# Mamba layer of a four-layer tower: two of sixteen state weightings moved to GpSimd, with their sums taken two places later

## The reference

```python
dbl = u @ xproj_w.T
delta = jax.nn.softplus(dbl[..., :DT_RANK] @ dt_w.T + dt_b)
A = -jnp.exp(A_log)
def step(hst, ins):                      # along the sequence
    d_t, B_t, C_t, u_t = ins
    dA = jnp.exp(d_t[..., None] * A)
    hst = dA * hst + (d_t * u_t)[..., None] * B_t[:, None, :]
    y = jnp.einsum('bds,bs->bd', hst, C_t)
    return (hst, y)
y = y + u * Dp
return (y * jax.nn.silu(z)) @ out_w.T
```

## Time and profile before

| | us |
|---|---|
| median of three runs | 3469.69 |
| lowest and highest run | 3464.54, 3469.84 |
| the profiled execution's own time | 3465.39 |
| its span | 3463.6 |
| the scan loop of the stage (first scan to last weighting) | 654.65 to 1364.65 |
| VectorE busy in the whole span | 2402.1 (69%) |
| TensorE busy in the whole span | 2484.2 (72%) |
| ScalarE, GpSimd busy in the whole span | 1594.3, 830.5 |
| mean granted TensorE clock | 0.826 of full speed |

### The profile page before, as it was taken

The page is one execution under the profiler, slowest core; times in us unless marked ns, Lnnn a source line. Parts: engine busy times, 40 slices in busy tenths (PEclk is TensorE's granted clock), DMA queues, the critical chain, the costliest instruction groups (busy, mean ns, idle before and its releaser), DMA issues. The chain is left out here.

```text
span 3463.6 us, 38446 instructions
## 1 busy us (share of the span) xinstructions
PE 2484.2 (72%) x12628; PEld 1541.3 (44%) x12668; DVE 2402.1 (69%) x5684; ACT 1594.3 (46%) x2912; POOL 830.5 (24%) x414
## 2 busy tenths in 40 slices
PE   4967995788888887589951112588889778885457
PEld 4964663333434333379840111322222456674335
DVE  5464336399999998411268998688888699999531
ACT  3111112566666662211215774577878455554211
POOL 2000000477777774167500000000000011111022
PEclk9868997799999998699965555799999887787578
DMA  1121001101011110411100000144435400000221
GB/s 53 19 83 46 1 1 32 78 21 66 33 49 49 49 49 0 148 49 40 64 12 0 1 0 2 62 146 152 146 118 187 126 1 1 1 1 1 86 112 54
DMA packets 81794, 185.36 MB, mean 54 GB/s; under 512 B 35197, under 2 KB 52827, under 8 KB 76251
## 3 DMA queue, kind: packets, MB, share of 16 engines
q1 hardware_dynamic: 75452, 170.66, 14.8%
q0 software_dynamic: 6144, 12.25, 1.1%
HBM read 166.00 MB, written 24.77 MB: 55 GB/s over the span
## 5 line engine op out<-in xcount | busy, mean ns | idle before, releaser
L2072 POOL TENSOR_TENSOR mam_st<-mam_du,mam_b_rows 128x1536 f32<-128x1536 f32 x128 | 439.5, 3441 | 172.9 <-PE mam_ysum L2141 172.3
L2302 DVE TENSOR_TENSOR_SCAN mam_st<-mam_da,mam_st 128x512 f32<-128x512 f32 x384 | 441.1, 1204 | 35.9 <-ACT mam_da L2242 18.2
L2141 PE MATMUL mam_ysum<-mam_st,held_ident 128*128 128x512 f32 x768 | 390.0, 648 | 2.2 <-DVE mam_st L2308 2.2
L1708 ACT ACTIVATE cod_hp<-cod_up,cod_b 128x512 f32<-128x512 f32 x512 | 316.7, 703 | 83.6 <-PE cod_up L1569 83.5
L2242 ACT ACTIVATE mam_da<-mam_delta,mamw_decay 128x508 f32<-128x508 f32 x384 | 254.2, 683 | 184.2 <-DVE mam_st L2302 149.6
L2423 POOL TENSOR_TENSOR att_probs<-att_se,att_neg 128x1536 f32<-128x1536 f32 x16 | 55.1, 3442 | 933.1 <-DVE att_neg L2628 933.1
L2308 DVE TENSOR_TENSOR mam_st<-mam_st,mam_c_ps 128x1536 f32<-128x1536 f32 x128 | 224.4, 1753 | 16.9 <-PE mam_c_ps L2136 13.4
L2141 PEld LDWEIGHTS mam_ysum<-mam_st,held_ident 128*128 128x128 f32 x768 | 159.2, 207 | 168.2 <-issue 161.1
L552 DVE SCALAR_TENSOR_TENSOR held_h<-x_dn,held_gate,held_h 128x192 f32<-128x192 f32 x256 | 89.1, 411 | 183.2 <-PE x_dn L519 181.5
L2628 DVE MATCH_REPLACE8 att_neg<-att_top,att_neg 128x128 f32<-128x128 f32 x768 | 201.1, 276 | 0.0
L1850 DVE TENSOR_TENSOR cod_hp<-cod_hp,cod_gate 128x512 f32<-128x512 f32 x256 | 163.5, 679 | 46.5 <-ACT cod_hp L1708 45.9
(11 more groups left out here) (533 smaller groups left out, 5528.8 us busy)
## 6 DMA issues: line engine op xcount, KB each, us to landing
cod_wide_gates<-gate_scratch SPq DMA_DIRECT2D x128, 512.0 KB, 3.9
mam_b_rows<-b_scratch SPq DMA_DIRECT2D x32, 1024.0 KB, 7.5
slot_scratch<-in_slot_fresh SPq DMA_DIRECT2D x2, 3860.0 KB
sw_w<-in_L_w SPq DMA_DIRECT2D x1, 6144.0 KB
gr_w<-in_L_w SPq DMA_DIRECT2D x1, 5376.0 KB
gr_w<-in_L_w SPq DMA_DIRECT2D x1, 4608.0 KB
sw_w<-in_L_w SPq DMA_DIRECT2D x1, 4608.0 KB
gr_rows<-slot_scratch SPq DMA_DIRECT2D x40, 96.5 KB, 2.0
```

The costliest lines, as they stand in the source:

```text
L1708: nc.scalar.activation(hp[step % HOLD][:, j, :], up[u % BANKS][:], ACT.Gelu_apprx_tanh, bias=b1[:, sub * HT + f:sub * HT + f + 1]).then_in ...
L2072: nc.gpsimd.tensor_tensor(st[it % N_ST][:], du[r % 2][:], along(b_rows[:, p % RING, n % PIECE, :], 1, [P, MC, MT]), ALU.mult)\
L2141: last = nc.tensor.matmul(ysum[:, c, :], m.ident[:], st[it % N_ST][:, c, :], start=False, stop=(it % DS == DS - 1))
L2302: nc.vector.tensor_tensor_scan(fs, fa, fs, 0.0, ALU.mult, ALU.add).then_inc(scanned, 1)
```

## The change

In each round turns 1 and 9 (`on_pool`: `it % 8 == 1`) are no longer weighted by VectorE. GpSimd weights them, in place, right behind the drive that is three turns on (POOL_LAG), with the row C(n) read from SBUF: SP loads it on all partitions into `c_rows`, a ring of two, from the scratch, which now holds 32 rows (C and B) of each round. TensorE leaves out `spread_c` for these turns and takes their sums two places later (SUM_LAG): the sums of turns q, q + 1, q + 2 come in the order q + 1, q + 2, q. The state buffers become five, and the ring of B pieces five.

```diff
-RING = 6
-N_ST = 4
+RING = 5
+C_RING = 2
+POOL_EVERY, POOL_AT, POOL_LAG, SUM_LAG = 8, 1, 3, 2
+N_ST = 5
+def on_pool(it):
+    return it % POOL_EVERY == POOL_AT
+def sum_place(it):
+    at = it % POOL_EVERY - POOL_AT
+    return it + SUM_LAG if at == 0 else it - 1 if 0 < at <= SUM_LAG else it
+def sum_turn(place):
+    at = place % POOL_EVERY - POOL_AT
+    return place - SUM_LAG if at == SUM_LAG else place + 1 if 0 <= at < SUM_LAG else place
...
         def _(sp):
...
                     sp.wait_ge(drive_ready, DS * (r - 1))
-                sp.dma_start(m.b_scratch[r % 2], dbl[B_ROW:B_ROW + DS, :]).then_inc(b_out, 16)
+                    sp.wait_ge(pool_weighted, DS // POOL_EVERY * (r - 1))
+                sp.dma_start(m.b_scratch[r % 2], dbl[0:B_ROW + DS, :]).then_inc(b_out, 16)
...
+                    if q % (POOL_EVERY // PIECE) == 0:
+                        k = p * PIECE // POOL_EVERY
+                        if k >= C_RING:
+                            sp.wait_ge(pool_weighted, k - C_RING + 1)
+                        sp.dma_start(c_rows[:, k % C_RING, :], m.b_scratch[r % 2, q * PIECE + POOL_AT, :]
+                                     .partition_broadcast(P)).then_inc(c_row_in[k % C_RING], 16)
...
         def _(pool):
+            def weight(it):
+                q, x = it // POOL_EVERY, st[it % N_ST]
+                pool.wait_ge(scanned, MC * (it + 1))
+                pool.wait_ge(c_row_in[q % C_RING], 16 * (q // C_RING + 1))
+                nc.gpsimd.tensor_tensor(x[:], x[:], along(c_rows[:, q % C_RING, :], 1, [P, MC, MT]), ALU.mult)\
+                    .then_inc(pool_weighted, 1)
...
-                        pool.wait_ge(summed, it - N_ST + 1)
+                        pool.wait_ge(summed, sum_place(it - N_ST) + 1)
...
+                    if it >= POOL_LAG and on_pool(it - POOL_LAG):
+                        weight(it - POOL_LAG)
...
         def _(pe):
...
             def spread_c(it):
                 r, n = it // DS, it % DS
-                pe.wait_ge(weighted, it)
+                if on_pool(it):
+                    return
+                pe.wait_ge(weighted, dve_count(it))
...
             def sums(it):
-                pe.wait_ge(weighted, it + 1)
+                wait_weighted(pe, it)
...
                     if it:
-                        sums(it - 1)
-            sums(NIT - 1)
+                        sums(sum_turn(it - 1))
+            sums(sum_turn(NIT - 1))
...
         def _(v):
...
             def weight(it):
+                if on_pool(it):
+                    return
                 v.wait_ge(scanned, MC * (it + 1))
-                v.wait_ge(c_ready, it + 1)
+                v.wait_ge(c_ready, dve_count(it) + 1)
```

More of the change, by code:

```diff
@@ L1950, in uses_before, with pool_count, dve_count @@
     return sum(USES[:r])
+def on_pool(it):
+    return it % POOL_EVERY == POOL_AT
+def pool_count(it):
+    return (it + POOL_EVERY - 1 - POOL_AT) // POOL_EVERY
+def dve_count(it):
+    return it - pool_count(it)
+def sum_place(it):
[4 more added lines that the diff above has]
+    return place - SUM_LAG if at == SUM_LAG else place + 1 if 0 <= at < SUM_LAG else place
 def conv_use(r):
@@ L1973, in mamba_stage @@
         b_rows = s.sb("b_rows", [P, RING, PIECE, MT])
+        c_rows = s.sb("c_rows", [P, C_RING, MT])
         st = [s.sb(f"st{i}", [P, MC, MT]) for i in range(N_ST)]
@@ L1989, in mamba_stage, with wait_weighted @@
         piece_in = [s.sem(f"piece_in{i}") for i in range(RING)]
+        c_row_in = [s.sem(f"c_row_in{i}") for i in range(C_RING)]
+        pool_weighted = s.sem("pool_weighted")
         n_w = 10
         block = s.block()
+        def wait_weighted(eng, it):
+            if on_pool(it):
+                eng.wait_ge(pool_weighted, pool_count(it + 1))
+            else:
+                eng.wait_ge(weighted, dve_count(it + 1))
         def wait_pre(eng, g):
@@ L2029, in _ @@
                     sp.dma_start(b_rows[:, p % RING].rearrange("p n t -> p (n t)"),
-                                 m.b_scratch[r % 2, q * PIECE:(q + 1) * PIECE, :]
+                                 m.b_scratch[r % 2, B_ROW + q * PIECE:B_ROW + (q + 1) * PIECE, :]
                                  .rearrange("n t -> (n t)").partition_broadcast(P)).then_inc(piece_in[p % RING], 16)
+                    if q % (POOL_EVERY // PIECE) == 0:
[4 more added lines that the diff above has]
+                                     .partition_broadcast(P)).then_inc(c_row_in[k % C_RING], 16)
         @block.gpsimd
@@ L2080, in _ @@
                             pool.wait_ge(drive_ready, it + 1)
+                            pool.wait_ge(pool_weighted, pool_count(it - POOL_LAG + 1))
                             c_lowest(r + 1)
@@ L2085, in _ @@
                             to_du(r + 1)
+            for it in range(NIT - POOL_LAG, NIT):
+                if on_pool(it):
+                    weight(it)
         @block.tensor
@@ L3360, in tower @@
         m.scratch = nc.dram_tensor("heads_scratch", [NB, H0, P, HD0], F32).ap()
-        m.b_scratch = nc.dram_tensor("b_scratch", [2, DS, MT], F32).ap()
+        m.b_scratch = nc.dram_tensor("b_scratch", [2, 2 * DS, MT], F32).ap()
         m.gate_scratch = nc.dram_tensor("gate_scratch", [2, 2, HT, ET, QD, GT], F32).ap()
```

## The result

The changed kernel takes 3537.95 us (median of 4 runs, 3533.55 to 3543.58) against 3467.11 for the kernel before in the same comparison (4 runs). The ratio is 1.0206, with a 95% interval of 1.0193 to 1.0218. The direction was forecast, the size was not: +71 us against +36.5, outside the stated range.

The account below looks back on a forecast made before the run. VectorE was taken to bound the stage, with TensorE and ScalarE adding waits. Reordered sums +28.0 us at full clock and clock +8.5 gave +36.5 on 3465.4, 3501.9; adjusted towards the median, 3504 was stated, range 3483 to 3527.

Parts of the forecast that it names:

- (1): Rival: TensorE's waits are made up for and VectorE's freed slots count, giving 3445 us; 8 in 100.
- (4): Rival: gains and stalls cancel because reordered sums seldom bind or waits coincide, 3465 to 3475 us; 5 in 100.
- the clock term: Sums in half of 12 chains without preparation slowed by TensorE's lower clock: +8.5 us, bounds 0 and 17.
- (a): Turn 1 of rounds 2, 4, 6: chains with convolution and projection lengthen, +9.3 us; in round 0 +0.5.
- (b): Turn 9, even rounds: saving lost waiting for ScalarE's decays; output chains lengthen in rounds 2, 4, 6, +16.6 us.
- (c): Turn 1 of rounds 1, 3, 5: TensorE's chain bounds up to the projection, +3.3 us each, +9.9 together.
- (d): Turn 9 of rounds 1, 3, 5: no preparation behind step 10, so a gain, -5.0 us.
- (e): Round 7, which prepares nothing: both GpSimd turns save VectorE time, -3.3 us.
- Rival 2: Clock falls in the filled chains too: 3544 us with all chains low, 3527 for half; 13 in 100.
- its estimate of 14 us: The clock cost if sums in the chains without preparation ran at a full half rate, 5.14 us each.
- rival 3: GpSimd late in odd rounds, one weighting per round delaying the scans: 27.5 us more, 3529; 8 in 100.
- rival 1: VectorE's freed slots count: 26.7 us less four places ScalarE holds (6.7), giving 3445 us; 8 in 100.

Follow-up runs that it names:

- e1: Changed kernel with only its order of sums kept: VectorE weights every turn, GpSimd none, no C rows loaded; 3549.8 us.
- e2: Changed kernel with no sums drawn forward: step q+1 adds nothing, q+2 adds turn q+1, q+3 adds turns q+2 and q; 3462.7 us.
- e10: Changed kernel with SUM_LAG 1 for 2, so the sums come in the order q+1, q; 3512.4 us.
- e3: Changed kernel with 9 to 18 products of zeros on TensorE ahead of the waiting sums in steps q+1 and q+2; 3507.1 us.
- e7: Kernel before the change with only five state buffers and a ring of five B pieces; 3468.3 us.
- e8: e2 with six state buffers and a ring of four pieces; 3459.1 us.
- e5: Changed kernel with TensorE's preparation put ahead of the waiting sums in steps q+1 and q+2; 3502.1 us.

## Why the prediction was right and wrong

**The mechanism was right.** The named place (TensorE idle ahead of the sums of turns 2, 3, 10, 11, released by the weighting), the chain that follows, and the direction are shown by the profile and by e1, e2 and e10. The rival by which VectorE's freed slots count (1) and the one by which gains and stalls cancel (4) did not come.

**The step that failed is the clock term**, +8.5 us with bounds 0 and 17. It rested on two choices: that only the 12 chains without preparation could fall, and only half of them would; the 20 filled chains were put at nothing. What was measured from weighting to weighting, against the kernel before, in us (e3 holds the clock up):

| part, over the stage | forecast, full clock | e3 | the change |
|---|---|---|---|
| (a) turn 1 of rounds 2, 4, 6 | +9.3 | +9.7 | +19.7 |
| (a) turn 1 of round 0 | +0.5 | +0.4 | +4.5 |
| (b) turn 9 of rounds 2, 4, 6 | +16.6 | +17.7 | +21.9 |
| (b) turn 9 of round 0 | 0 | +0.6 | +3.1 |
| (c) turn 1 of rounds 1, 3, 5 | +9.9 | +10.4 | +15.5 |
| (d) turn 9 of rounds 1, 3, 5 | -5.0 | -5.4 | +2.6 |
| (e) round 7 | -3.3 | -3.6 | +3.4 |
| sum | +28.0 | +29.8 | +70.7 |

Each row sums W(0) to W(4), W(8) to W(12), W(0) to W(7) or the whole round. The clock is the last column less the one before, 41 us, where 8.5 stood. Some 17.5 of it lie in the chains with nothing in them (round 0 at turn 9, rows d and e), where 9 of 12 ran low, and 23.4 in the filled ones, where 14 of 20 did. The 23 groups of sums at 4.46 us for 2.68 make the same 41. Against the kernel before the profile also has 1.7 us of waits for late drives more (turn 15 of rounds 1, 3, 5) and 4.5 less in the closing products.

Why it was missed, as I see it: the low clock of the earlier trace rows was read as a matter of stretches with little work, and a mean clock of 0.94 to 0.96 in the earlier trace rows as a sign that the filled chains were safe. But those means came from TensorE working through without a wait. The change puts in front of every reordered sum a wait of 1.9 to 4.5 us, and the sums are the first work behind it: at turn 1 of rounds 2, 4 and 6 they run at 0.61 of full speed twice in a row, although the first chain holds 6 us of work to 2 of waiting. Rival 2 named this at 13 in 100, with 3527 for half of the filled chains' 34 us and all of the empty ones' 17; its sign, sums of over 4 us in the filled chains, is what came (4.37). But it was held unlikely because I weighed the busy share over a chain instead of asking what stands right behind the wait. Its full price, 3544, is close to what came, 3538, in part by luck: it has all 32 chains low where 23 were.

The Trainium skill (TensorE: Matmul & The Clock Gate, Part 1: The HAM clock gate) states that an idle array falls back to half rate. The trace agrees: 5.28 us for six sum matmuls behind 4.28 us of waiting, granted clock 0.50, against 2.57. That alone does not say which waits do it: behind 1.92 us the trace has 0.61 and 1.00. My text set its estimate of 14 us aside for the rows' 8.5; what kept both small was the count, six chains where 23 ran low.

**Parts.** Right: the freed slot of turn 9 in the even rounds is lost to ScalarE (S(10) waits 3.79 us for the decays instead of 2.00). GpSimd's weighting costs 3.44 us (median 3436 ns of 16) and is hidden; the rings cost nothing (e7), and no wait for a row C shows in the trace: GpSimd's 16 weightings waited 5.5 us in all, for VectorE's scans. The drives are late by 0.66 us once a round in rounds 1, 3, 5, 2 us in all, and not as rival 3 had it (27.5). GpSimd's weighting lies ahead of the row, at 816.34; what pushes the row back is drive 14, which waits for the late sums of turn 9:

```profile
833.70 3.44 POOL L2119 TENSOR_TENSOR mam_st<-mam_du,mam_b_rows 128x1536 f32<-128x1536 f32 x1 [3.21 <-PE mam_ysum L2196]
```

Wrong with the clock: (d) and (e) as gains.

**The result's other half.** What the freed slots are worth without the sums drawn forward is shown by e8: 9.6 us of the stage, not 26.7, nor the some 20 of rival 1. ScalarE holds those of turn 9 in the even rounds, and TensorE, with the sums it was already full of, those of turn 1 in the odd ones.

## What to carry to other kernels

When work is reordered on an in-order engine, write down the chain from one use of the scarce buffer to the next, and count the work that now stands between the wait and the next release; a wait that was last in its step costs nothing, the same wait in the middle costs all that stands behind it. Give the TensorE work right behind each new wait a price at the low clock, however busy the engine is on average: here 23 of 32 such groups paid it, behind waits of 1.9 us and more, and no run shows how to tell them from the nine that did not. A late result can be added late without drawing anything forward. Independent work belongs ahead of a wait if it is ready itself: at turn 1 of the even rounds it filled the wait and the sums ran at full clock, while the output products of e5 waited themselves and gained nothing.

## What the runs showed of the hardware that was not expected

A wait of 1.92 us, after 15 us of unbroken work and with 8 us of work behind it, was enough for the next sums to run at a granted clock of 0.61 (4.37 us instead of 2.57), and the clock was back at 1.00 for the convolution that followed. Products of zeros in the wait (e3) hold it up: the sums behind them last 2.84 us, with the same data and the same start behind the weighting, so it was the standing idle ahead of them that cost the clock. But the same 1.92 us of waiting left it at 1.00 ahead of the sums at 827.98, and in e10 at 863.06; what decides between the two stays open. At 820.14 the sums of one turn took 5.28 us at 0.50, the longest seen.
